# Moving the FFN weight loads from the GpSimd queue to the SyncE queue and the final combine from VectorE to GpSimd

## The reference

```python
xn = layernorm(x)                                # rows, no affine part
q, k, v = split(xn @ w_qkv.T, 3)                 # 512 wide each
s = softmax(causal(q @ k.T / sqrt(512))) @ v     # attention, one head
s = s @ w_out.T + b_out                          # 2048 x 1024
wg, wu, wd = w_gate / 127, w_up / 127, w_down / 127   # int32 weights, hidden size 3072
h = silu(xn @ wg.T) * (xn @ wu.T)                # 2048 x 3072
g = silu(h @ wd.T)                               # 2048 x 1024
out = x + s * g
```

## Time and profile before

| | us |
|---|---|
| median of 3 runs | 1832.58 |
| lowest and highest of them | 1831.58, 1943.67 |
| the profiled execution | 1832.32 |
| span of its slowest core, core 2 | 1830.7 |
| spans of the eight cores | 1812.8 to 1830.7 |
| mean granted TensorE clock of the cores | 0.957 to 0.967 |

### The profile page before, as it was taken

How to read it: one execution, slowest core, us unless ns; L and a number is a source line. 1 busy time by engine, 2 the same in 40 slices (tenths; PEclk the granted TensorE clock), 3 DMA queues, 4 the chain that set the end, 5 groups by cost and what they waited for, 6 DMA issues and landing times.

```text
span 1830.7 us, 20554 instructions; the slowest of 8 cores (1812.8 to 1830.7 us)
## 1 busy us (share of the span) xinstructions
PE 1624.9 (89%) x7748; PEld 772.2 (42%) x7748; DVE 458.9 (25%) x740; ACT 257.8 (14%) x415; POOL 227.3 (12%) x304
## 2 busy tenths in 40 slices
PE   4788799968888888699999899999899999899995
PEld 3555544434444443344434344444344444344442
DVE  5333222132222222133300332301333201333102
ACT  2323211122222222001100101000110001010001
POOL 0000000000000000122211122211122211222110
PEclk9888899979999999899999999999999999999998
DMA  4112010015444420432322522322532323432223
GB/s 141 35 35 70 1 35 12 1 58 103 93 93 103 94 69 24 115 77 74 93 64 75 184 71 79 90 67 75 183 79 71 87 75 117 136 81 75 60 73 126
DMA packets 45649, 146.17 MB, mean 80 GB/s; under 512 B 6321, under 2 KB 14769, under 8 KB 44978
## 3 DMA queue, kind: packets, MB, share of 16 engines
q0 software_dynamic: 23808, 94.39, 21.2%
q1 hardware_dynamic: 21170, 48.38, 7.9%
q10 hardware_dynamic: 576, 2.10, 0.3%
HBM read 146.94 MB, written 35.65 MB: 100 GB/s over the span
## 4 chain that ended last, share of the span: by engine, by line
PE 78%; DMA 8%; DVE 6%; ACT 4%; issue 3%; DVEq 1%; ACTq 0%; SPq 0%; POOL 0%; POOLq 0%
PE psA L247 54%; PE psA L943 7%; PE psB L676 5%; DMA wdb<-wdb_scr 4%; PE psB L742 4%; PE psB L943 3%; PE psC L943 3%; DMA xin<-x 2%; DVE xnT_lo L448 1%; DMA wub<-wub_scr 1%; DVE otl L976 1%; DVE otl L973 1%; DMA wof_st<-woutT 1%; ACT oaT_hi L700 1%; ACT oaf L682 1%
## 5 line engine op out<-in xcount | busy, mean ns | idle before, releaser
L247 PE MATMUL psA<-xnT_hi,wgb 128*128 128x512 f16 x768 | 295.8, 385 | 34.0 <-DVEq L1009 17.2
L247 PE MATMUL psA<-xnT_lo,wgb 128*128 128x512 f16 x768 | 295.6, 385 | 0.0
L247 PE MATMUL psA<-xnT_hi,wub 128*128 128x512 f16 x768 | 291.1, 379 | 0.0
L247 PE MATMUL psA<-xnT_lo,wub 128*128 128x512 f16 x768 | 291.1, 379 | 0.0
L859 DVE SCALAR_TENSOR_TENSOR hfs<-psA,hsc 128x512 f32<-128x512 f32 x96 | 66.4, 692 | 442.8 <-PE psA L247 439.0
L79 POOL DMA_DIRECT2D wgb<-wgb_scr x96 | 85.1, 886 | 626.4 <-PE psA L247 527.5
L851 ACT ACTIVATE hsc<-psA,zeroc 128x512 f32<-128x512 f32 x96 | 66.0, 687 | 592.2 <-PE psA L247 550.7
L943 PE MATMUL psA<-wdb,hT_hi 128*128 128x512 f16 x384 | 116.4, 385 | 21.1 <-DVEq L1009 11.9
L247 PEld LDWEIGHTS psA<-xnT_hi,wgb 128*128 128x128 f16 x768 | 76.0, 99 | 131.4 <-issue 44.6
L943 PE MATMUL psA<-wdb,hT_lo 128*128 128x512 f16 x384 | 117.2, 388 | 0.0
L973 DVE TENSOR_TENSOR otl<-sin,gtl 128x1024 f32<-128x1024 f32 x16 | 19.6, 1226 | 389.4 <-ACTq L1009 356.9
(11 more groups left out here) (112 smaller groups left out, 1823.1 us busy)
## 6 DMA issues: line engine op xcount, KB each, us to landing
wgb<-wgb_scr POOLq DMA_DIRECT2D x96, 256.0 KB, 3.9
wub<-wub_scr POOLq DMA_DIRECT2D x96, 256.0 KB, 4.1
wdb<-wdb_scr POOLq DMA_DIRECT2D x96, 256.0 KB, 2.9
xt<-x SPq DMA_DIRECT2D x16, 512.0 KB, 3.9
sscr<-stl SPq DMA_DIRECT2D x16, 512.0 KB, 3.9
sin<-sscr SPq DMA_DIRECT2D x16, 512.0 KB, 6.3
xin<-x SPq DMA_DIRECT2D x16, 512.0 KB, 8.2
out<-otl SPq DMA_DIRECT2D x16, 512.0 KB, 4.3
```

The costliest lines, as they stand in the source:

```text
L247: k.op("te", lambda e, lf=lf, rf=rf, j=j, n=n, pf=psum_ap_fn: e.matmul(pf(), lf(), rf(), start=(j == 0), stop=(j == n - 1)), inc=(inc if j ...
```

## The change

All loads of `wgb`, `wub` and `wdb` are issued by SP in place of POOL, at the same places of the program. The combine's multiply and add move from DVE to POOL, with a semaphore of their own, `gq`, for which ACT and SP now wait where they waited for DVE's. Two waits at the head of POOL's FFN list go away with the loads.

SP's list then reads, slab for slab: (in slab 0: gate and up loads 0 and 1), gate and up loads 2 to 23, with `wdb` 0 and 1 behind load 23; `sin` and `xin` for tt = 0 and 1; gate and up loads 0 and 1 of the next slab; `wdb` 2 to 23; then the four waits for the combine with the stores of `out` and the loads of `sin` and `xin` for tt = 2 and 3; and then the next slab's gate and up load 2.

```diff
@@ semaphores @@
-              "dF0", "dF1", "dD0", "dD1", "pe", "ve", "se"):
+              "dF0", "dF1", "dD0", "dD1", "pe", "ve", "se", "gq"):
@@ head of the FFN @@
     k.wait("sy", "ve", ve_p2_done)
     k.wait("sy", "dG", 16 * 12)
-    k.wait("gp", "ve", ve_p2_done)
-    k.wait("gp", "dG", 16 * 12)
@@ emit_gu_load @@
         if pe_gu_use.get(h % 2) is not None:
-            k.wait("gp", "pe", pe_gu_use[h % 2])
-        k.dma("gp", lambda h=h: wgb.ap()[:, h % 2],
+            k.wait("sy", "pe", pe_gu_use[h % 2])
+        k.dma("sy", lambda h=h: wgb.ap()[:, h % 2],
               lambda h=h: wg_r[:, :, h * 128:(h + 1) * 128], f"dF{h % 2}")
-        k.dma("gp", lambda h=h: wub.ap()[:, h % 2],
+        k.dma("sy", lambda h=h: wub.ap()[:, h % 2],
               lambda h=h: wu_r[:, :, h * 128:(h + 1) * 128], f"dF{h % 2}")
@@ wdb 0 and 1, at h == NH - 2 @@
-                        k.wait("gp", "pe", pe_wd_use[hh0])
-                    k.dma("gp", lambda hh0=hh0: wdb.ap()[:, hh0],
+                        k.wait("sy", "pe", pe_wd_use[hh0])
+                    k.dma("sy", lambda hh0=hh0: wdb.ap()[:, hh0],
@@ emit_sx_load @@
             if ve_comb.get(tt % 2) is not None:
-                k.wait("sy", "ve", ve_comb[tt % 2])
+                k.wait("sy", "gq", ve_comb[tt % 2])
@@ wdb 2 to 23 @@
-                    k.wait("gp", "pe", pe_wd_use[h % 2])
-                k.dma("gp", lambda h=h: wdb.ap()[:, h % 2],
+                    k.wait("sy", "pe", pe_wd_use[h % 2])
+                k.dma("sy", lambda h=h: wdb.ap()[:, h % 2],
                       lambda h=h: wd_r[:, h, :], f"dD{h % 2}")
@@ combine, for tt in range(4) @@
             if ve_comb.get(tt % 2) is not None:
-                k.wait("se", "ve", ve_comb[tt % 2])
+                k.wait("se", "gq", ve_comb[tt % 2])
...
-            k.wait("ve", "se", se_gtl[tt])
-            k.wait("ve", dl_tt[tt][0], dl_tt[tt][1])
+            k.wait("gp", "se", se_gtl[tt])
+            k.wait("gp", dl_tt[tt][0], dl_tt[tt][1])
             if out_n >= 2:
-                k.wait("ve", f"dO{out_n % 2}", 16 * (out_n // 2))
-            k.op("ve", lambda e, tt=tt, gb=gb: e.tensor_tensor(
+                k.wait("gp", f"dO{out_n % 2}", 16 * (out_n // 2))
+            k.op("gp", lambda e, tt=tt, gb=gb: e.tensor_tensor(
                 otl.ap()[:, tt % 2, :], sin.ap()[:, tt % 2, :], gb.ap(), ALU.mult))
-            k.op("ve", lambda e: e.drain())
-            k.op("ve", lambda e, tt=tt: e.tensor_tensor(
+            k.op("gp", lambda e: e.drain())
+            k.op("gp", lambda e, tt=tt: e.tensor_tensor(
                 otl.ap()[:, tt % 2, :], otl.ap()[:, tt % 2, :], xin.ap()[:, tt % 2, :],
                 ALU.add))
-            k.drain_inc("ve", "ve")
-            ve_comb[tt % 2] = k.cnt["ve"]
-            ve_comb_last = k.cnt["ve"]
-            k.wait("sy", "ve", ve_comb[tt % 2])
+            k.drain_inc("gp", "gq")
+            ve_comb[tt % 2] = k.cnt["gq"]
+            ve_comb_last = k.cnt["gq"]
+            k.wait("sy", "gq", ve_comb[tt % 2])
```

## The result

| | before | after |
|---|---|---|
| median of 42 runs of each, us | 1835.04 | 1845.54 |
| ratio to before, with its 95% interval | | 1.0058 [1.0037, 1.0079] |
| the slowest core's span, us | 1830.7 (core 2) | 1838.9 (core 3) |
| mean of the eight spans, us | 1822.6 | 1834.1 |

The changed kernel is 10 us slower, 0.6%: a small difference, but the interval does not hold 1. It is what is left of two larger sums of opposite sign.

A forecast was written before the change was run, and what follows sets the result against it. PE, busy 89% of the span, was taken to bound the kernel, so only its waits could change. Terms -5.8 - 8 - 1 + 21.8 + 6.0 = +13.0 on 1832.3 us gave 1845 us, range 1820 to 1880.

The forecast's parts named there:

- Part 1: Gate and up loads in steady state: a pair lands in 3.8 to 5.4 us, hidden by PE's step; change 0.
- Part 2: First gate and up load at the FFN's start: goes out ahead of the sin and xin loads, -5.8 us.
- Part 3: Down parts: SP's shorter issue and landing of wdb loads ends PE's stalls, -8 us, ends 11.4 and 0.
- The sign: Down parts, what would show it: wdb waits near 0 and PE's idle time down to 3 or 4 us.
- Part 4: DVE's cast between gate and up and down parts: quicker without POOL's issues beside it, three times 0.35, -1 us.
- Part 5: Three passages between slabs: next slab's gate and up load 2 waits behind all four combines on SP, +21.8 us.
- S: Start of a slab's first combine, from which the passages and the end are timed; PE's restart forecast at S + 28.5.
- The rivals on a slow or a quick POOL operation: Combines on POOL: operation of 4.9 us gives 1917 us, chance 0.12 for slow; 1.23 us gives 1825, chance 0.13 for quick.
- the factor of three: Passages and end: one combine's time enters three times into each, 12 times in all.
- Part 6: The kernel's end: combine 3 ends 22.05 us after the first combine's start in place of 16.06, +6.0 us.
- a gain over 2%: Rival for the whole kernel: every PE wait taken away, 36 us in all; chance 0.03.

The follow-up runs named there:

- experiment 5: Kernel before, with SP holding the sin and xin loads in slab 0 until PE ended the last gate and up step: ratio 0.9986 to before.
- experiment 1: Kernel before, with only the wdb loads moved to SP: ratio 0.9877 to before.
- experiment 4: Changed kernel, with each combine's multiply made twice on POOL: ratio 1.0212 to the kernel before.
- Experiment 10: Changed kernel, with gate and up loads 2 and 3 ahead of the waits for combines 2 and 3, last slab's combine on DVE: ratio 0.9862 to before.
- experiment 8: Kernel before, all weight loads on SP, combines and stores of tt = 2 and 3 put behind the next slab's steps 1 and 2: 1798.48 us, ratio 0.9803.
- 11: Kernel before, all weight loads on SP, combines of tt = 2 and 3 put off into the next slab, measured a second time: 1796.97 us, ratio 0.9778.
- experiment 3: Kernel before, with the combine moved to POOL and all weight loads left on POOL: ratio 1.0226 to before.
- experiment 7: Changed kernel, with POOL itself issuing the out stores and the sin and xin loads for tt = 2 and 3: ratio 0.9993 to the kernel before.
- experiment 12: Kernel before, combines of tt = 2 and 3 put off into the next slab, all weight loads left on POOL: ratio 1.0017 to before.
- experiment 2: Kernel before, with all weight loads on SP and the combine left on DVE: ratio 0.9886 to before.

## Why the prediction was right, and where its terms were not

The forecast of 1845 us was met by the median of 1845.54, and the sign and the reason were right: the load half gains, the wait that the combine half puts into SP's list costs more. But the sum was +13.0 against +8.2 in the profiled executions, and two of its terms were off by 13 and 8 us in opposite directions. The means of all cores put these two misses at 7 and 5 us, again in opposite directions. The base moved too: the sum stood on an execution of 1832.3 us, and the kernel before has a median of 1835.04 over 42 runs. The agreement within 1 us is luck; what was forecast well is the sign and the reasons.

**Part 1, steady state: right.** PE waits on `wub` only at the FFN's start and in the three passages. A pair lands some 4.4 us after its first issue (medians: 0.4 us between the issues and 4.0 from the second to its landing), inside the 3.8 to 5.4. In a stretch of 100 us of steady steps, 780 to 880, PE is without a gap, and the queue line of its loads, 30 before and 29.5 after, reads (packets, MB, share of 16 engines):
```profile
q0 software_dynamic: 2390, 7.86, 30.9%
```
```profile
q1 hardware_dynamic: 30656, 7.73, 34.4%
```
That is 1.03 and 1.17 us of engine time for a load, 13% more. The rows of the load are the same; the packets are a sixteenth as long, 256 bytes where POOL's queue has 4096. The Trainium skill, page DMA: Bandwidth & Descriptors, section Specifications, asks for 512 bytes a transfer to reach line rate; the trace has packets of 256 bytes and shows only these 13%, far from what would bring a step over its 6.91 us.

**Part 2, the first load: right** (-5.4 for -5.8, -5.1 in the mean), and experiment 5 shows its cause.

**Part 3, the down part: the term was mis-sized,** -21.2 on the ledger's two cores and -15.4 in the mean of eight, where it said -8 with an end at -11.4. The direction and the mechanism (a shorter cycle on SP) are shown by experiment 1. The sign came out, too: the idle time in the last table below is 0.7 us, where 3 or 4 had been named. The step that failed is that I took the listed waits, 7.1 us, and the idle time of the stage table, 11.4 us, for all that PE loses. A pair of matmuls is drawn 0.59 us long, while the next pair starts after 0.43. A late pair first fills those 0.16 us unseen, and only the rest is listed: ahead of the pair at 959.59 in the earlier trace rows stands this one:
```profile
958.72 0.59 PE L943 MATMUL psC<-wdb,hT_lo 128*128 128x512 f16 x2
```
The next is due at 959.15 and comes at 959.59, 0.44 late, with 0.28 listed. The chain shows it without any model. Every second step of before, then single steps of after (start us, length, what):
```profile
952.24 1.89 PE psA L943 x8
959.59 1.89 PE psA L943 x8
966.87 1.89 PE psA L943 x8
```
```profile
957.46 1.73 PE psA L941 x8
960.91 1.73 PE psA L941 x8
964.36 1.73 PE psA L941 x8
```
Two steps take 7.28 to 7.35 us before and 2 x 3.45 = 6.9 after: some 0.35 to 0.4 a time (0.5 in the last part), at most twelve times in each of four parts, up to 19 us. The same in the stage table, cut tightly around the 384 matmuls of each part, sum of the four, before and after:
```profile
sum 357.75, PE 348.48; mean PE 87.12
```
```profile
sum 336.80, PE 336.13; mean PE 84.03
```
Of the 21 us between them 12.4 had stood under "busy". Not all of it is waiting for loads. From the starts of the matmuls against a pitch of 0.216 us the four parts lost some 26 us before and some 5 after. Of these 21 some 17 are stalls, and some 4.6 are first steps at the lower clock: eight matmuls take 2.8 to 3.6 us at the start of all four down parts before, and 2.7 and 2.9 in two of four after, 1.9 in the others. The latter does not go with the change. Over all eight cores 28 of 32 down parts start at the lower clock before, 24 of 32 after and 29 of 32 in experiment 1, and one such start costs some 1.65 us, so they make under 1 us of the mean's 15.4. The part's first matmul waits as long for DVE in both (10.8 us in four, and 11.9 before).

**Part 4, DVE's cast: right** in size, -1.0 with all the rest of the gate and up parts.

**Part 5, the passages: right in its mechanism, mis-sized by 7.7 us,** +29.5 for +21.8 (+26.6 in the mean of eight cores). In the first passage PE restarts at S + 31.6 and not at S + 28.5. Step by step: combine 0 ends at S + 5.8 (forecast 5.0), because POOL's first combine has 1.14 us between its operations, which no later one has. `xin` takes 7.3 us to land where I had put the row's minimum, 6.1, though its median of 8.2 stood beside it; combine 2 starts at S + 14.3 (12.05). Combines 2 and 3 take 11.05 us (10.0), since POOL and DVE hold each other up for about a microsecond and not for 0.3. From the end of combine 3 it is then 6.3 us to PE's start (6.45), 5.7 of them from the pair's issue. In passages 2 and 3 it is 30.9 and 31.0, there through an `xin` of 7.9 and 8.0 us. A single POOL operation was priced at 2.4 us and takes 2.34. The Trainium skill, GPSIMD Engine Reference, section Performance versus the Vector engine, has 4497 ns for 2048 elements, half of which is an estimate of 2.25; the trace is 4% above it. The rivals on a slow or a quick POOL operation are thus out, and experiment 4 shows the factor of three by which it would have counted.

**Part 6, the end: right,** +7.4 for +6.0 (+6.2 in the mean), the difference again `xin` (7.4 us to land for 6.1). Experiment 10 takes 5 to 6 of it back by DVE.

**What the prediction had not weighed** is the order as such. It said "SP's order forbids it" of a gain over 2%, and this holds for the change as made. Experiments 8 and 11 have the loads on SP too, but the combine on DVE and another order, and gain 2.0 and 2.2%. Nor had it weighed the clock: a passage in which PE hardly stops saves some 2 us more in the gate and up part behind it (experiment 8).

## What to carry to other kernels

Before you put the work of two queues into one, write down the merged list and look for the first instruction that PE waits for, and for what now stands ahead of it; an engine change that looks like relief (combine off DVE) is worth nothing while the list that feeds PE waits for the same work. Put the old slab's tail behind the loads and the first steps of the new one in every list at once, not in one. And to size a stall of PE, measure from start to start of repeated steps against an undisturbed pitch: listed waits and idle time leave out what the modelled ends cover, here over half. And do this on more than the slowest core: with the slowest core of each kernel the down parts seem to gain 21 us, over all cores it is 15.

## What the runs showed of the hardware

- With POOL's own loads ahead, the gap at a drain between two of its operations is long: 2.3 to 2.95 us some 6 us after the last load's issue (experiment 3), and 3.2 to 5.8 us right behind a store and two loads (experiment 7). Behind a store alone it is 0.23 us in most cases (experiment 7, tt = 3), and with no issue ahead 0.14 us, but for 1.14 in the changed kernel's very first combine. That makes POOL a poor place for short work behind its own loads.
- A multiply or add of 128x1024 in f32 takes 2.34 us on POOL and 1.23 on DVE. When both work on SBUF at a time both suffer: the subtraction on DVE (L863 of the changed kernel), 0.69 us alone, took 2.67 beside POOL's operations, and these took 2.57 to 2.89. The Trainium skill, SBUF — State Buffer, section Who interferes with whom, says that a DVE instruction with two SBUF inputs contends with a GpSimd instruction that reads SBUF; the trace agrees, and for such a pair it shows the cost on both sides.
- DVE's cast (L863 of the kernel before, L861 of the changed one), 0.77 us in the median while POOL issues a pair in every step, has a median of 0.43 us once SP issues them.
- A 256 KB load of 1024 rows is issued by SP in 0.36 us and by POOL in 0.88. When loads queue up, SP's issue grows: the median of `wub` is 0.58 us and the longest 4.58.
- Two queues do not shield their transfers from each other: a gate and up pair took 9.2 to 13.0 us to PE's start beside four 512 KB loads on the other queue and 5.8 to 6.3 us without them (experiment 5, eight cores), and was late in the same way in steady state (experiment 12, 3.2 to 4.7 us of waiting on cores 0 to 3).
- After a pause of 6.04 us PE got a granted clock of 0.79 over its next 10 us; after one of 0.16 us it kept 1.00 (experiment 8), and on core 0 the three gate and up parts behind the passages took 154.8 us each, where those of experiment 2, after pauses of 7.7 to 8.2 us, took 156.4 to 157.6.
